# Softmax sums loaded broadcast and inverted as 128x512 in an attention + mixture-of-experts layer

## What is computed

```
x = x + attention(layernorm(x))        # 16 heads of 16, causal softmax, W_qkv, W_out, biases
y = layernorm(x)
x = x + (y + sum over the 2 best of 8 experts of share_e * (gelu(norm(y) @ w1[e] + b1[e]) @ w2[e] + b2[e]))
# softmax: attn = exp(scores) / sum(exp(scores)); out = attn @ v
```

## Time and profile before

| what | value |
|---|---|
| median of 3 runs | 971.73 us (963.93 to 974.81) |
| the profiled execution, whole | 968.54 us |
| its span, first to last instruction | 966.7 us |
| mean granted TensorE clock in it | 0.927 of full |
| busy in the span: TensorE, VectorE, ScalarE, GpSimd | 845.1, 727.1, 587.1, 466.3 us |
| DMA | 130.09 MB in 146327 packets |

### The profile page before, as it was taken

The page is one execution under the profiler, slowest core; times in us unless marked ns, Lnnn a source line. Parts: engine busy times, 40 slices in busy tenths (PEclk is TensorE's granted clock), DMA queues, the critical chain, the costliest instruction groups (busy, mean ns, idle before and its releaser), DMA issues.

```text
span 966.7 us, 21226 instructions
## 1 busy us (share of the span) xinstructions
PE 845.1 (87%) x6870; PEld 567.3 (59%) x6870; DVE 727.1 (75%) x1658; ACT 587.1 (61%) x1079; POOL 466.3 (48%) x565
## 2 busy tenths in 40 slices
PE   4899977868888978787787899999999999999996
PEld 3455523323343525242242689889888988889875
DVE  6677878876759797988986588786776776666664
ACT  1676557655768787876868464665545554455453
POOL 4000023324435676756486657774476554445441
PEclk9899978777697979899897999999999999999999
DMA  9788658654766868566734751442323332332321
GB/s 203 226 290 281 215 153 234 204 127 125 192 190 205 211 174 213 155 191 175 203 110 136 234 138 27 68 96 49 47 45 53 53 56 45 51 50 47 42 50 18
DMA packets 146327, 130.09 MB, mean 135 GB/s; under 512 B 59344, under 2 KB 128848, under 8 KB 146096
## 3 DMA queue, kind: packets, MB, share of 16 engines
q1 hardware_dynamic: 115648, 87.51, 32.5%
q0 software_dynamic: 15680, 18.95, 12.4%
q10 hardware_dynamic: 14896, 22.28, 7.1%
HBM read 83.63 MB, written 44.80 MB: 133 GB/s over the span
## 4 chain that ended last, share of the span: by engine, by line
PE 40%; DVE 15%; DMA 13%; issue 11%; POOL 10%; SPq 6%; ACT 3%; POOLq 1%; ACTq 0%; DVEq 0%
PE banks L770 12%; PE banks L788 11%; PE banks L583 5%; POOL out L1704 4%; DMA weighed_values<-arena 3%; POOL slot_tokens L1651 3%; PE banks L686 2%; DVE arena L1231 2%; POOL arena L1680 2%; DVE weights L1385 2%; PE banks L573 2%; PE banks L698 2%; PE banks L642 2%; SPq L1782 2%; DMA inverse_sums<-arena 2%
## 5 line engine op out<-in xcount | busy, mean ns | idle before, releaser
L992 ACT ACTIVATE arena<-banks,arena 128x256 f32<-128x256 f32 (+1 forms) x312 | 152.5, 541 | 172.4 <-issue 125.5
L770 PE MATMUL banks<-arena,weights 128*128 128x256 f16 (+1 forms) x1872 | 204.4, 265 | 3.0 <-DVE arena L1487 2.4
L788 PE MATMUL banks<-weights,arena 128*128 x1704 | 193.8, 273 | 0.5 <-DVE arena L1515 0.5
L770 PEld LDWEIGHTS banks<-arena,weights 128*128 x1872 | 173.9, 98 | 28.5 <-issue 4.9
L1704 POOL DMA_INDIRECT out<-arena x71 | 116.2, 1636 | 150.1 <-DVE arena L1526 111.9
L788 PEld LDWEIGHTS banks<-weights,arena 128*128 128x128 f16 x1704 | 165.6, 98 | 20.5 <-issue 1.3
L642 PE MATMUL banks<-arena 64*128 64x128 f16 (+3 forms) x512 | 120.7, 336 | 35.6 <-DMA arena<-arena 12.6
L614 PE MATMUL banks<-arena 62*128 62x384 f16 (+3 forms) x512 | 97.6, 332 | 36.1 <-DVE arena L1228 10.6
L1513 DVE TENSOR_SCALAR arena<-arena 128x512 f16<-128x512 f32 (+1 forms) x156 | 76.2, 489 | 60.4 <-ACT arena L992 58.8
L1515 DVE SCALAR_TENSOR_TENSOR arena<-arena 128x512 f16<-128x512 f32 (+1 forms) x156 | 110.1, 706 | 5.6
L642 PEld LDWEIGHTS banks<-arena 64*128 64x128 f16 x512 | 38.6, 100 | 118.4 <-issue 37.8
(11 more groups left out here) (191 smaller groups left out, 1333.9 us busy)
## 6 DMA issues: line engine op xcount, KB each, us to landing
weights<-in_L_ffn_w ACTq DMA_DIRECT2D x16, 1024.0 KB, 7.7
arena<-in_L_ffn_w SPq DMA_DIRECT2D x32, 512.0 KB, 4.4
qk_parts<-weights SPq DMA_DIRECT2D x64, 128.0 KB
arena<-qk_parts SPq DMA_DIRECT2D x128, 64.0 KB, 3.4
weighed_values<-arena SPq DMA_DIRECT2D x32, 256.0 KB
token_rows<-arena SPq DMA_DIRECT2D x12, 512.0 KB, 5.0
arena<-qk_parts SPq DMA_DIRECT2D x128, 32.0 KB, 3.6
arena<-weighed_values SPq DMA_DIRECT2D x32, 128.0 KB
```

The lines of the kernel that those rows point to most:

```text
L770: m = pe.matmul(bank[:, c * TILE:c * TILE + WIDTH[j]], w1[:, k, wp, f:f + P], xp[:, k, 0:WIDTH[j]], start=(i == 0), stop=(i == len(terms) ...
L788: m = pe.matmul(bank[:, c * D:(c + 1) * D], hp[:, f, c * P:(c + 1) * P], w2[:, f // (FC // 2), wp, f % (FC // 2), :], start=(f == 0 and i ...
L992: m = act.activation(h_32[r % 2][:, c, 0:WIDTH[j]], banks[:, 1 + c2, c * TILE:c * TILE + WIDTH[j]], ACT.Gelu, bias=b1_now[j % 2][:, 2 * c2 ...
```

## The change

The reciprocal no longer goes through DRAM. `move_o` now loads, beside the weighed values, the sixteen equal rows of sums of each head into a second full tile `o_over[k]` (64 partitions x 512 elements per unit, the same partitions as the values). `invert` takes the reciprocal of a whole `o_over[k]`, 128x512, in place, once for two units. `divide` waits for that alone and multiplies. `keep_inverse`, `move_inverse`, `inverse_dram`, `sums` and `o_inverse` are gone. `move_o` now waits for the last `out_proj` of the batch before, as `o_over` is its operand.

The timetable moves too. `invert` is at +92 and `divide` at +97 ticks after the end of the second unit (before +102 or +110, and +156 or +164; the last two units +120 and +124, before +130 and +216). The batch chain of every batch begins 74 ticks sooner, that of the last batch, which had 78 extra ticks and now has 40, 112 ticks sooner. `move_o` of a batch's first unit is 16 ticks later, `with_bias` relative to its base 20 ticks sooner, and `place` of the first three batches is spread over 24 ticks per tile instead of 12.

```diff
@@ -128,7 +128,6 @@
         qk_dram = dram("qk_parts", (2, B, H, 2, HD, T), F16)
         v_dram = dram("v_rows", (B, T, H, HD), F32)
         o_dram = dram("weighed_values", (2, P, T), F32)
-        inverse_dram = dram("inverse_sums", (2, HG, T), F32)
         rows_dram = dram("token_rows", (N + P, ROW), F32)
         acc_dram = t["out"]
         slots_dram = dram("slot_tokens", (E * N, 1), I32)
@@ -198,8 +197,7 @@
         assert LENT == late_dram.shape[0] and LENT * HALF == 3 * EW // 2
         o_raw = a2.take(T)
         o_dense = [a2.take(T) for _ in range(KC)]
-        o_inverse = [a2.take(T) for _ in range(KC)]
-        sums = [a2.take(HG * TT) for _ in range(2)]
+        o_over = [a2.take(T) for _ in range(KC)]
         turned = a2.take(KC * T, k=KC, t=T)
         x2 = a2.take(TT * D, t=TT, d=D)
         rows = a2.take(TT * D, t=TT, d=D)
@@ -332,14 +330,10 @@
 
             late = u >= UNITS - 2
             at(after + 51, "keep_o", u)
-            at(after + (84 if late else 70), "move_o", u)
-
-            room = 8 if u < 6 else 0
-            at(after + (130 if late else 102 + room), "invert", u)
-            at(after + (136 if late else 112 + room), "keep_inverse", u)
-            at(after + (176 if late else 136 + room if u % NG else 158 + room), "move_inverse", u)
+            at(after + (84 if late else 70 if u % NG else 86), "move_o", u)
             if u % 2 == 1:
-                at(after + (216 if late else 156 + room), "divide", divmod(u // 2, KC))
+                at(after + (120 if late else 92), "invert", divmod(u // 2, KC))
+                at(after + (124 if late else 97), "divide", divmod(u // 2, KC))
         for i in range(len(matrices) - EARLY):
             at(i * 36 + 30, "load_weights", i + EARLY)
             at(i * 36 + 92, "magnitude", (i + EARLY, 0))
@@ -368,10 +362,10 @@
         at(UNITS * UNIT + 3, "gelu_table", 0)
         ranked_at = {}
         for b in range(B):
-            base = (b + 1) * NG * UNIT
+            base = (b + 1) * NG * UNIT - 74
             at(base + 142, "load_again", b)
-            at(base + 186, "with_bias", b)
-            base += 78 if b == B - 1 else 8
+            at(base + 166, "with_bias", b)
+            base += 40 if b == B - 1 else 8
             for half in range(2):
                 at(base + 175 + 12 * half, "out_proj", (b, half))
                 at(base + 181 + 12 * half, "copy_out", (b, half))
@@ -408,7 +402,7 @@
                 at(base + 478 + 3 * step, "rank", (b, step))
             at(base + 505, "shares_out", b)
             for tt in range(TT):
-                at(base + 506 + 12 * tt, "place", (b, tt))
+                at(base + 506 + (24 if b < B // 2 - 1 else 12) * tt, "place", (b, tt))
             ranked_at[b] = base + 496
         for i, (batches, _, _, _) in enumerate(PARTS):
 
@@ -695,7 +689,7 @@
                 for s in range(2):
                     tt = 2 * half + s
                     for k in range(KC):
-                        m = pe.matmul(bank[:, s * D:(s + 1) * D], o_inverse[k][:, tt * P:(tt + 1) * P], w_out[:, k, :],
+                        m = pe.matmul(bank[:, s * D:(s + 1) * D], o_over[k][:, tt * P:(tt + 1) * P], w_out[:, k, :],
                                       start=(k == 0), stop=(k == KC - 1))
                 m.then_inc(sem("side_made"), 1)
 
@@ -1234,11 +1228,10 @@
                     m = v.tensor_reduce(out[:, :, slot // 2, 0], pair[:, :, 3 * P:T], AX.X, ALU.max, negate=True)
                 m.then_inc(sem("maxed"), 1)
 
-            def invert(u):
-                w.wait_ge(sem(f"o_moved{u % 2}"), 32 * (u // 2 + 1))
-                if u >= 2:
-                    w.wait_ge(sem(f"inverse_kept{u % 2}"), 16 * (u // 2))
-                v.reciprocal(sums[u % 2], sums[u % 2]).then_inc(sem("inverted"), 1)
+            def invert(b, k):
+                for half in range(2):
+                    w.wait_ge(sem(f"o_moved{half}"), 32 * (KC * b + k + 1))
+                v.reciprocal(o_over[k], o_over[k]).then_inc(sem("inverted"), 1)
 
             def add_out(b, half):
                 w.wait_ge(sem("with_bias"), b + 1)
@@ -1547,7 +1540,7 @@
                     if later < UNITS:
                         maxima(later, slot)
                 elif stage == "invert":
-                    invert(n)
+                    invert(*n)
                 elif stage == "magnitude":
                     magnitude(n[0], n[1:])
                 elif stage == "find_scales":
@@ -1636,10 +1629,8 @@
                 g.tensor_tensor(top_part[:, :, 1], top_small, top_part[:, :, 0], ALU.subtract).then_inc(sem("top_split"), 1)
 
             def divide(b, k):
-                for half in range(2):
-                    w.wait_ge(sem(f"inverse_moved{half}"), 16 * (KC * b + k + 1))
-                    w.wait_ge(sem(f"o_moved{half}"), 32 * (KC * b + k + 1))
-                g.tensor_tensor(o_inverse[k], o_dense[k], o_inverse[k], ALU.mult).then_inc(sem("o_divided"), 1)
+                w.wait_ge(sem("inverted"), KC * b + k + 1)
+                g.tensor_tensor(o_over[k], o_dense[k], o_over[k], ALU.mult).then_inc(sem("o_divided"), 1)
 
             def place(b, tt):
                 w.wait_ge(sem("slots_known"), b + 1)
@@ -1803,31 +1794,12 @@
                 k, half = divmod(g, 2)
                 if b > 0:
                     w.wait_ge(sem("o_divided"), KC * (b - 1) + k + 1)
+                    w.wait_ge(sem("side_made"), side_made("out_proj", (b - 1, 1)))
                 w.wait_ge(sem("o_kept"), 16 * (u + 1))
-                if u >= 2:
-                    w.wait_ge(sem(f"inverse_kept{u % 2}"), 16 * (u // 2))
                 heads = o_dram[u % 2].rearrange("(h s) t -> h s t", h=HG)
-                sp.dma_start(o_dense[k][HG * HD * half:HG * HD * (half + 1), :], heads[:, 0:HD, :]).then_inc(
-                    sem(f"o_moved{u % 2}"), 16)
-                sp.dma_start(sums[u % 2], heads[:, HD, :].rearrange("h (a c) -> h a c", c=HG * TT)).then_inc(
-                    sem(f"o_moved{u % 2}"), 16)
-
-            def keep_inverse(u):
-                w.wait_ge(sem("inverted"), u + 1)
-                if u >= 2:
-                    w.wait_ge(sem(f"inverse_moved{u % 2}"), 16 * (u // 2))
-                sp.dma_start(inverse_dram[u % 2].rearrange("h (a c) -> (h a) c", c=HG * TT), sums[u % 2]).then_inc(
-                    sem(f"inverse_kept{u % 2}"), 16)
-
-            def move_inverse(u):
-                b, g = divmod(u, NG)
-                k, half = divmod(g, 2)
-                w.wait_ge(sem(f"inverse_kept{u % 2}"), 16 * (u // 2 + 1))
-                if b > 0:
-                    w.wait_ge(sem("side_made"), side_made("out_proj", (b - 1, 1)))
-                sp.dma_start(o_inverse[k][HG * HD * half:HG * HD * (half + 1), :],
-                             inverse_dram[u % 2].unsqueeze(1).broadcast_to([HG, HD, T])).then_inc(
-                    sem(f"inverse_moved{u % 2}"), 16)
+                for into, first_row in ((o_dense[k], 0), (o_over[k], HD)):
+                    sp.dma_start(into[HG * HD * half:HG * HD * (half + 1), :], heads[:, first_row:first_row + HD, :]).then_inc(
+                        sem(f"o_moved{u % 2}"), 16)
 
             def load_raw(i, e_, m_, k_):
                 if raw_before[i] is not None:
...
```

More of the change, by code:

```diff
@@ L1910, in sync @@
                     move_o(n)
-                elif stage == "keep_inverse":
-                    keep_inverse(n)
-                elif stage == "move_inverse":
-                    move_inverse(n)
                 elif stage == "store_weights":
```

## The result

| | before | changed |
|---|---|---|
| median, us | 969.26 (963.93 to 974.81) | 1065.45 (1060.58 to 1070.9) |
| ratio, 95% interval | | 1.099 (1.094 to 1.103) |
| span of the profiled execution, us | 966.7 | 1058.8 |
| first to last `copy_o` (attention), us | 148.2 to 544.6: 396.4 | 145.1 to 639.5: 494.4 |
| last `copy_o` to the end, us | 422.1 | 419.3 |

What follows compares the result with a forecast made beforehand. The prediction took VectorE as the fullest engine, setting the pace in four attention batches, with TensorE bounding the expert stage. +17 + 4 - 8 = +13 us on 971.7 gave 985 us, range 960 to 1005.

Steps and rivals of the forecast that it cites:

- What VectorE's work costs by itself: In four full attention batches from 301.2 us, wide reciprocals add 6.0 us each; with VectorE 93% busy, +17 us.
- TensorE is held there by the maxima behind the same `invert`, so the two waits are one: At `out_proj` behind `divide`: no wait beyond that for the maxima, so no cost; otherwise 1.3 us more.
- The wait in front of `invert`: VectorE waiting for `move_o`'s loads: 1 us in each of four full batches, +4 us; upper bound +39.
- My own sign of being wrong: The prediction is wrong if L1241, the reciprocal, waits over 20 us for its loads in attention.
- The gain of 8 us: In early attention, removing the inverse's DRAM way and SP's waits gives -8 us, bounds 0 and -39.
- SP's new wait: `move_o` waits for the previous batch's `out_proj`, delaying `load_unit` and `keep_o`: a microsecond or two if TensorE is late.
- The shift of the chain: Batch 6's earlier chain work falls where VectorE has room; batch 7's `out_proj` stays in the expert stage: no gain.
- Edits that cost nothing: The step costing `divide`'s new wait, `out_proj`'s place, `move_o`'s new wait and the earlier chain at nothing.
- The expert stage: From the last `copy_o` to the end: the distance should stay at 422 us within 3.

Runs made afterwards that it cites:

- e5: The kernel before plus a 3.2 us VectorE reduction that nothing waits for at each of the sixteen new places of `invert`; 981.3 us, ratio 1.013.
- e3: The changed kernel with each reciprocal taking only the first 16 of 512 columns, timetable untouched; 1033.6 us, ratio 1.066.
- e1: The changed kernel with its batch chain begun 37 ticks sooner in place of 74; 1045.2 us, ratio 1.080.
- e2: The changed kernel with its batch chain begun 56 ticks sooner in place of 74; 1050.6 us, ratio 1.082.
- e8: The changed kernel with two pairs of tiles for the sums, chain 37 ticks sooner in place of 74, `invert` and `divide` 20 ticks later; 1033.9 us.
- e16: e11 with each reciprocal taking only the first 16 of 512 columns; 967.9 us, ratio 0.997.
- e6: The changed kernel with a second pair of tiles for the sums, so `move_o` skips waiting for the previous batch's `out_proj`, except in the last batch; 1067.9 us.
- e17: The changed kernel with `gate` and `copy_gate` alone 12 ticks sooner; 1043.1 us, ratio 1.075.
- e15: e8 with `gate` and `copy_gate` 12 ticks sooner; 1003.0 us, ratio 1.036.
- e12: The kernel before with its batch chain 37 ticks sooner, the last unit's `move_inverse` and `divide` earlier to make room; 1047.3 us, ratio 1.080.
- e14: e11 with `out_proj` and `copy_out` alone 11 ticks later; 996.0 us, ratio 1.030.
- e13: The changed kernel with its batch chain 48 ticks sooner, one whole unit, in place of 74; 1010.6 us, ratio 1.044.
- e11: e8 with the batch chain 48 ticks sooner, one whole unit, in place of 37; 993.8 us, ratio 1.023.
- e18: e11 with `gate` and `copy_gate` 12 ticks sooner; 986.0 us, ratio 1.015.
- e4: e1 with each reciprocal taking only the first 16 of 512 columns; 1010.6 us, ratio 1.044.

## Why the prediction was wrong

- **What VectorE's work costs by itself**, +17, was if anything too high: 10 to 12 us in e5, whose interval of 5 to 20 doesn't exclude it. VectorE reached 94 to 96% in e5's full batches, where I took 93%, and at most 81% in a batch of the changed kernel. In its place in the chain the width is worth 32 us (e3). The step that I called the dearest, a full VectorE, is not where the 96 us are.
- **"TensorE is held there by the maxima behind the same `invert`, so the two waits are one"** is the step that failed first. They are not one: TensorE was idle for 9.65 us ahead of one `out_proj`, 50.1 us in 7, beside 27.7 us for the maxima; I had costed it at nothing with 1.3 us a batch as the bound. The cause is plain from the chain: 17 ticks are 4.6 us of timetable (at 13 us a unit), and the reciprocal and `divide` alone are 4.6 us, so that any lateness of the loads passed straight to TensorE. With that room given back the kernel is only 20 (e1) and 15 us (e2) faster, as the lateness then stands in front of the maxima. I had every number of this sum, and laid it beside a wait for the maxima in place of adding it up.
- **The wait in front of `invert`**, +4, was mis-sized: 39.0 us in 9 waits against 17.6. I had bound it at 39 and taken a tenth of that. The load took 8.18 us from issue to landing in the chain above, where I had 4.9 us for the narrow one. e8 shows that 11 us hang on it in another place. My own sign of being wrong, more than 20 us of this wait, came.
- **The gain of 8 us** from the way through DRAM and SP is not there. The first three stretches grew, from 41.5, 59.6 and 51.9 us to 48.2, 66.4 and 69.1, where I had the first two 8 us shorter. e16 stands at 0.997 of before. SP's new wait, which I put at a microsecond or two, was 60.2 us, but taking three quarters of it away gave nothing (e6).
- **The shift of the chain** I looked at for how much work falls beside which, never for the order it makes between two stages of different batches on one queue. "Edits that cost nothing" has no term for it, and `gate` is in no step of the prediction. It is worth 22 us in the changed kernel (e17) and 31 at a shift of 37 (e15), and the kernel before with its chain moved 37 ticks lost 78 (e12).
- **The clock** had no term. The granted clock in attention fell from 0.85 to 0.80 (windows view over the whole of it), and TensorE's busy time rose from 315.6 to 350.0 us for the same instructions: a third of the 98 us lost in attention. The fastest runs had more of it (0.84 in e14 and e5, 0.87 in e16), but not in step: e1 had 0.83 at 1045 us and e15 0.80 at 1003. Whether the clock is a cause of its own or follows the stands is not shown.
- **The expert stage** was right: 419 us behind the last `copy_o`, 422 within 3.

The parts don't add up to 96, as each hides behind the next: the width is worth 32 us (e3), the gate 22 (e17), one unit's place with the room that it gives `out_proj` 55 (e13), the stand of SP nothing (e6). What is shown is the way from 1065 down: 1011 (e13), 994 with 20 ticks more for the loads and two pairs of tiles (e11), and from there either 986 with the gate (e18) or 968 with short reciprocals (e16). Open is by what path `gate` acts, why the place within a unit costs 17 us more with the gate moved in both (e15 against e18), and how e12's loss divides between its two waits.

## What to carry to other kernels

When a stage moves along a timetable written by hand, write down for each queue which two stages it now stands between, and add up the shortest chain from its last input to its first reader in microseconds, against the ticks that are left; a margin of zero hands every late load to the engine that reads last. Where a stage of the next batch waits for one of the batch before (here `copy_out` for `gate`), try the earlier batch's stage further ahead on its queue: it gave 6 to 31 us in four kernels. Work on an engine at 85% that nothing waits for was cheap (10 to 12 us for 53); the same work inside the chain cost 26 to 35 (e16, e3, e4).

## What the runs showed of the hardware

```profile
406.30:410.00 3.70, 3.65 (x12) 2.60 (x16) 0.91 (x1) 0.00 (x0) 3.07 (x5) 0.53 0.02 2
```

In before the same eight products at 429.97 us took 1.95 us at 1.00. Over attention, with stalls of 4 to 10 us once a batch, the mean duration of `out_proj`'s 128x256 product rose from 433 to 576 ns, and the mean granted clock fell from 0.85 to 0.80 of the full 2.4 GHz.
